# A GNN and mixture-of-experts kernel on one core: nine tiles' fetches and one store moved ahead of the last chunk's scatters

## The reference, cut to what matters

```
x = x + gnn(layernorm(x), src, dst, W, b)      # sum over edges of normed rows, @ W, scaled, relu
x = x + ffn(layernorm(x), Wr, ..., W1, W2)     # below

probs = softmax(xt @ Wr + br); top_p, top_idx = top_k(probs, 2)
weights = top_p / top_p.sum()
h = gelu(xe @ W1[e] + b1[e]); y = h @ W2[e] + b2[e]        # for each expert e
out = sum over the two chosen experts of weights * y
```

## Time and profile before

| | before |
|---|---|
| time, median of 3 runs | 1611.21 us (1607.22 to 1613.84) |
| profiled execution: its time | 1615.5 us |
| profiled execution: its span | 1613.9 us |
| POOL busy | 1157.6 us, 72% of the span |
| PE busy | 1165.9 us, 72% |
| DVE busy | 1026.4 us, 64% |
| DMA bytes | 381.53 MB, mean 236 GB/s |

### The profile page before, as it was taken

One profiled execution on the slowest core, in us unless ns is written; L12 is line 12 of the kernel. 1 busy time (PEld: TensorE's weight loads), 2 busy tenths in 40 slices (PEclk: granted clock), 3 DMA queues, 4 the chain that ended last, 5 costly groups with the idle time before them and its releaser, 6 DMA issues. The chain is left out here.

```text
span 1613.9 us, 27049 instructions
## 1 busy us (share of the span) xinstructions
PE 1165.9 (72%) x9182; PEld 993.0 (62%) x9182; DVE 1026.4 (64%) x2810; ACT 644.6 (40%) x1273; POOL 1157.6 (72%) x1087
## 2 busy tenths in 40 slices
PE   6961657664761849879699696968949877898870
PEld 6961536452541838768588585856848766777760
DVE  8995767687682765847557575774756567556640
ACT  3974332133201424434245252423414453555660
POOL 8885777777777777777777777777777707677523
PEclk9999756576665979989899898987979999999995
DMA  8359878767667578787787787767768768899990
GB/s 279 116 180 341 295 257 277 256 223 238 227 190 253 172 243 275 219 257 239 229 271 242 254 260 221 241 224 234 227 207 248 233 183 248 231 286 280 306 284 8
DMA packets 258142, 381.53 MB, mean 236 GB/s; under 512 B 24339, under 2 KB 217479, under 8 KB 253780
## 3 DMA queue, kind: packets, MB, share of 16 engines
q1 hardware_dynamic: 192280, 232.69, 44.1%
q0 software_dynamic: 59360, 140.70, 30.1%
q10 hardware_dynamic: 6364, 6.40, 1.2%
HBM read 302.58 MB, written 80.08 MB: 237 GB/s over the span
## 5 line engine op out<-in xcount | busy, mean ns | idle before, releaser
L914 POOL DMA_INDIRECT gt<-zt,srcI x768 | 787.7, 1026 | 244.0 <-issue 179.5
L1313 PE MATMUL ps<-gt,S 128*128 128x257 f16 x1536 | 297.6, 318 | 181.0 <-DMA gt<-zt,srcI 168.0
L1431 PE MATMUL ps<-xe,w1b 128*128 128x256 f16 (+1 forms) x2736 | 332.0, 275 | 27.5 <-DVE xe L1891 18.5
L1313 PEld LDWEIGHTS ps<-gt,S 128*128 128x128 f16 x1536 | 190.9, 152 | 243.0 <-DMA gt<-zt,srcI 215.2
L1260 ACT ACTIVATE h<-ps,cb 128x256 f32<-128x256 f32 (+1 forms) x456 | 224.9, 543 | 283.9 <-PE ps L1431 270.6
L1446 PE MATMUL ps<-w2b,hT 128*128 128x256 f16 x2544 | 305.1, 278 | 14.8 <-DVE yb L1926 5.9
L1431 PEld LDWEIGHTS ps<-xe,w1b 128*128 128x128 f16 x2736 | 260.7, 102 | 70.6 <-DVE xe L1891 26.8
L1446 PEld LDWEIGHTS ps<-w2b,hT 128*128 128x128 f16 x2544 | 252.9, 100 | 51.1 <-issue 14.4
L1898 DVE SCALAR_TENSOR_TENSOR hT<-h,cb,hT 128x512 f16<-128x512 f32 (+1 forms) x228 | 161.0, 711 | 132.8 <-ACT hT L1264 130.5
L1264 ACT ACTIVATE hT<-h,cb 128x512 f16<-128x512 f32 (+1 forms) x228 | 157.8, 692 | 7.4
L943 POOL DMA_INDIRECT xs<-xrow,slI x98 | 100.9, 1030 | 74.1 <-DVE slI L1634 44.6
(11 more groups left out here) (292 smaller groups left out, 1493.3 us busy)
## 6 DMA issues: line engine op xcount, KB each, us to landing
w1b<-ws SPq DMA_DIRECT2D x57, 1024.0 KB, 6.6
w2b<-ws SPq DMA_DIRECT2D x57, 1024.0 KB, 8.8
ws<-w2b SPq DMA_DIRECT2D x16, 1024.0 KB, 5.6
xb<-xs SPq DMA_DIRECT2D x49, 260.0 KB, 8.3
gt<-zt,srcI POOLq DMA_INDIRECT x768, 5.3
ys<-yb SPq DMA_DIRECT2D x34, 256.0 KB, 9.4
zg<-zf SPq DMA_DIRECT2D x8, 1028.0 KB
gt<-zg SPq DMA_DIRECT2D x8, 1028.0 KB
```

The costliest lines, as they stand in the source:

```text
L914: e.indirect_dma_start(out=gt[:, i % NG, :], out_offset=None, in_=zt, in_offset=bass.IndirectOffsetOnAxis(ap=srcI[:, c, r:r + 1].bitcast(u ...
L1313: inst = e.matmul(PS[r % 2][:, 0:257], S[:, r % NS, :, c], gt[:, i % NG, part * 257:part * 257 + 257], start=(c == 0 and part == 0), stop= ...
L1431: inst = e.matmul(UP[n % 2][:, z * BS:z * BS + 128 * size(m)], w[:, l, kk, j * 128:(j + 1) * 128], xe[m % 2][:, k, kk, 0:128 * size(m)], s ...
```

## The change: what it does

Only `plan()` is changed, and the list that it makes. Every engine issues the same instructions as before; PE, ACT and SP also in the same order. POOL and DVE have theirs in another order from block 34 on.

- Fetches (`cg`) of tiles 0 to 8 may be listed before the last chunk's scatters; one `give` may too.
- `sums` costs the planner's POOL 2.0 instead of 1.3 for each tile, but the next `give` or `sums` is held for 13.0 after it; a `give` costs 1.9 a DMA and holds the next for 5.0 or 2.6.
- A fetch is taken to land 5.0 after its issue, not 2.0, before its `cc` is listed.
- No `cc` is listed before step `r5` of the last chunk, and a fetch isn't listed where it would hold up a `give` or `sums` that is due.

```
 def step_give():
-    if max(s["chain"], s["base"]) > s["now"] or clock["POOL"] > s["now"] + 2.6 or LAST not in sent:
+    if max(s["chain"], s["base"]) > s["now"] or clock["POOL"] > s["now"] + 2.6 or LAST not in sent and s["given"]:
         return False
     if batches and batches[0][0] <= s["now"]:
         b = batches.popleft()[1]
-        emit("sums", b, (("POOL", 1.3 * (SUMS[b][1] - SUMS[b][0])),), s["now"])
+        emit("sums", b, (("POOL", 2.0),), s["now"])
         s["summed"] += 1
+        s["chain"] = clock["POOL"] + 13.0
     elif gives and (BLOCKS[gives[0]][0] < LAST or s["late"] <= s["now"]):
-        emit("give", gives[0], (("POOL", 1.7 * GIVES[gives.popleft() - M0]),), s["now"])
+        k = GIVES[gives[0] - M0]
+        emit("give", gives.popleft(), (("POOL", 1.9 * k),), s["now"])
         s["given"] += 1
+        s["chain"] = clock["POOL"] + (5.0 if k > 1 else 2.6)
     else:
         return False
-    s["chain"] = clock["POOL"] + 5.0
     return True
...
-                if kind == "cg" and (clock["POOL"] > s["now"] + 2.5 or LAST not in sent):
+                if kind == "cg" and (clock["POOL"] > s["now"] + 2.5 or LAST not in sent and arg >= NC - 1):
+                    continue
+                if kind == "cc" and s["placed"] <= LAST:
+                    continue
+                if kind == "cg" and (gives or batches) and LAST in sent and max(clock["POOL"], s["now"]) + 2.6 > max(s["chain"], s["base"]) + 1.5:
                     continue
...
-                chain.at = end + 2.0 if kind == "cg" else s["now"] + 4.0 if kind in ("pl", "pw") else s["now"] + 1.5 if kind == "blanks" else s["now"] if kind == "xs" else end
+                chain.at = end + 5.0 if kind == "cg" else s["now"] + 4.0 if kind in ("pl", "pw") else s["now"] + 1.5 if kind == "blanks" else s["now"] if kind == "xs" else end
```

## The result

| | before | after |
|---|---|---|
| time, median of 17 runs each | 1612.0 us (1607.22 to 1620.02) | 1603.44 us (1598.32 to 1608.85) |
| ratio | | 0.9949, 95% interval 0.9935 to 0.9962 |
| profiled execution: its time, its span | 1615.5, 1613.9 us | 1605.4, 1603.8 us |
| last `sums` issued (span time) | 1535.50 | 1486.11 |
| last `give` issued | 1606.48 | 1595.05 |

The gain is real and small: 8.6 us at the median, where about 21 were forecast. In the profiled executions the last `sums` went 49.4 us earlier and the last `give` only 11.4.

The account below looks back on a forecast made before the run. Bound: POOL's list from 1346 to 1535, then `give` landings. Last `sums` at 1487.8, first `give` behind it at 1507.1, plus 45, 12.6 and 21.0 gives 1585.7; with 7.4 and 1.6, 1594.7 profiled, median about 1590, range 1573 to 1607.

Parts of the forecast that it names:

- Issue of the last `sums`: On POOL: fetches and `give`s moved away and shorter waits, less later scatters, bring it from 1535.50 to 1487.8.
- The scatters: On POOL, the last chunk's scatters: fetches and one `give` moved ahead delay them and all that follows by 8.5 us.
- the `give`s behind the first three `sums`: On POOL: more fetches stand ahead, so waits of 8.15, 3.65 and 3.81 us become 2.7, 0 and 0: -12.9 us.
- the 6.07: On POOL: the last `sums`' wait of 6.07 us for a `give`, forecast to stay, for another `give`.
- Its landing: Behind the last `sums`: 18.48 us to land, at 1506.3, and block 43's `give` 0.8 us later, at 1507.1.
- The step that failed: Queue behind the last `sums`: six large `give`s at 7.5 us each, 45 us, block 49's at 1552.1.
- Two small `give`s under load and five without: End of POOL's queue: two at 6.3 us with weights loading, five at 4.19; 12.6 and 21.0 us, to 1585.7.
- Span end behind the last `give`: End of the kernel: the span ends 7.4 us after the last `give`'s issue, as in the profile before.
- The second rival: Queue of `give`s only gets longer, large ones at 9.57 us: time 1611.7, median 1607; 0.19 together with no gain.
- Block 56: End of the block stream: done at 1581.5 instead of 1578.8, just before its turn in the queue of `give`s.
- the third rival: Fetches behind each of three `sums` stop the blocks, some 19.4 us each: time 1631.5, median 1627; chance 0.08.
- The first rival: `give`s behind the last `sums` keep up, so the last block sets the end: time 1582.3, median 1578; chance 0.20.

## Why the prediction was wrong

The direction was right, and so was the mechanism: the end stayed the queue of `give`s behind the last `sums`. What failed is the size of one term of the sum, the step of that queue under load. By its steps:

- **Issue of the last `sums`**: 1487.8 forecast, 1486.11 measured. The scatters were 6.1 us late (8.5), the `give`s behind the first three `sums` waited 0.30, 0.30 and 2.04 us (2.7, 0 and 0), the 6.07 became 3.99, and two waits were new, 1.23 and 1.65 us ahead of the second and third `sums`.
- **Its landing**: 17.0 us to the next `give` instead of 19.3, so block 43's went 4.0 us earlier than forecast.
- **The step that failed**, "I take the middle, 7.5, since fetches are over by then but weights still load: 6 x 7.5 = 45": the six took 59.2, so this term was 14.2 us too small. Each step measured 9.87 us, because a landing beside the weights took 6.9. The three rows that I took the middle of, 9.57, 7.48 and 5.36, differ by load, and the kernel before shows it in these three stretches (columns as in the earlier trace rows):

```profile
1554.70:1564.30 9.60, 9.05 (x84) 7.43 (x85) 2.89 (x10) 4.15 (x11) 3.22 (x2) 0.73 1.09 328
1564.30:1571.80 7.50, 6.74 (x88) 6.04 (x86) 4.08 (x12) 6.26 (x17) 3.13 (x3) 1.00 0.94 242
1571.80:1577.20 5.40, 4.21 (x39) 3.56 (x38) 2.87 (x12) 1.42 (x4) 3.15 (x3) 1.00 0.19 58
```

The shares were 1.09, 0.94 and 0.19. POOL had issued its last fetch at 1521.38, so fetches had no part in any of the three: what ended was the weight loads, the last two of which (`w2b`) SP issued from 1560.97 on. So "fetches are over by then but weights still load" described the row of 9.57 and not the middle, and the new place, with a share of 1.01 and 1.11, was like that row. With an eighth of the weights the step fell to 6.42.
- **Two small `give`s under load and five without**: 12.4 and 20.3 us (12.6 and 21.0).
- **Span end behind the last `give`**: 8.8 us (7.4).

These terms together: -1.7 - 2.3 + 14.2 - 0.2 - 0.7 + 1.4 = +10.7, and 1594.7 + 10.7 = 1605.4 is the profiled execution's time. The second rival was nearest, by its price of 9.57 for all six.

- **Block 56** was done at 1579.5 (1581.5). Behind the three `sums` DVE waited 6.0, 5.2 and 11.3 us, 22.5 in all where I took 18 and the third rival asked for 42. Among the small blocks PE waited 1.44 us at most, as forecast. But DVE's waits did not halve (38.2 of 47.1), since others stayed that I had taken as gone, the 6.2 at 1381.12 above all, and PE lost 11.0 us there. Block 38's load, which I had put 5 us later, was issued at 1355.36, 0.4 us later. So terms of this sum were wrong both ways, and that it came out near is partly luck.
- **The first rival** is refuted: no large `give` under load landed early enough for the queue to keep up with the blocks. The Trainium skill's DMA: Bandwidth & Descriptors, section Anatomy of one DMA, from which I worked out an estimate of 2.3 us for one landing, is not borne out for these accumulating DMAs: even with an eighth of the weights the least was 3.0 and the median 3.9.

Where the 49.4 us went, from block to block of the two timelines: the landing of the last `sums` gave 2.2 us more. The three `give`s that moved behind it (43 to 45) took 29.7 there (1503.14 to 1532.81). Those of 46 to 48 took 29.6 instead of 22.4, and from block 49's to block 56's it took 32.7 instead of 29.3, because more of them now ran while weights loaded. -49.4 - 2.2 + 29.7 + 7.2 + 3.4 = -11.3, which is the move of the last `give`, 11.4, but for rounding. In this kernel, moving work ahead of the queue gained nothing for the steps that the planner then put into the queue itself.

## What to carry to other kernels

Price a step of a serial chain by the load that will stand beside it in its new place, not by the middle of rows from other places: ask which stream makes the load, and until when that one runs. Where each DMA of a chain waits for the landing of the one before, look for a second chain: with the same bytes it took 17 us off here (in a kernel whose output lacks half of the late results, so it shows the price and is no finished version). Fewer and larger steps gained nothing that can be told, since their landings grew. Where the profile names an engine as the releaser, look up when that engine made this instruction's own data: here a count that had been reached long before was credited to the latest increment.

## What the runs showed of the hardware

The landing of an indirect accumulating DMA of 128 rows of 1 KB depended on the load more than I had expected, and not in proportion (one profile each): 3.9 us at the median with shares of 0.58 and 0.34 (98 and 75 GB/s), 4.4 with 0.79 and 0.72 (180 and 198 GB/s), 6.9 with 1.01 and 1.11 (269 and 337 GB/s). A plain accumulating DMA (`sums`) took longer with its size, but with a wide spread: 3 tiles landed in 10.3 us, 10 in 11.9 to 17.3 (six in the kernels before and after), 11 in 15.0, 16.3 and 18.5, 15 in 18.6 and 20.2, all in stretches with a share of 0.92 or more. From 3 to 15 tiles that is an estimate of (19.4 - 10.3) / 12 = 0.8 us a tile (19.4 is the mean of the two), on top of some 8, and single landings lie up to 4 us off it.
